# Turning a column of 256 numbers into a row: tensor-engine transposes replaced by a VectorE block transpose and two trips through DRAM

## What is computed

```python
# layer 0
h = relu(layernorm(x))
weight = adj * exp((h @ Wq.T + bq) @ (h @ Wk.T + bk).T)
weight = weight / weight.sum(axis=2, keepdims=True)
x = x + weight @ (h @ Wv.T + bv)
# layer 1
h = relu(layernorm(x))
A_hat = adj + eye
d_inv_sqrt = A_hat.sum(axis=-1) ** -0.5
L = A_hat * d_inv_sqrt[:, :, None] * d_inv_sqrt[:, None, :]
x = x + L @ (h @ W + b)
```

## Time and profile before

| | |
|---|---|
| median of 3 runs | 1750.32 us (1748.71 to 1751.24) |
| the profiled execution, its own time | 1750.99 us |
| its span in the trace, first to last instruction | 1749.1 us |
| TensorE busy | 1725.3 us (99%) |
| VectorE busy | 1266.5 us (72%) |
| ScalarE busy | 746.5 us (43%) |
| GpSimd busy | 555.7 us (32%) |
| DMA | 105.55 MB, mean 60 GB/s |
| mean granted TensorE clock | 0.997 of full speed |

### The profile page before, as it was taken

One profiled execution on the slowest core, in us unless ns is written; L12 is line 12 of the kernel. 1 busy time (PEld: TensorE's weight loads), 2 busy tenths in 40 slices (PEclk: granted clock), 3 DMA queues, 4 the chain that ended last, 5 costly groups with the idle time before them and its releaser, 6 DMA issues.

```text
span 1749.1 us, 32667 instructions
## 1 busy us (share of the span) xinstructions
PE 1725.3 (99%) x11452; PEld 1574.7 (90%) x11452; DVE 1266.5 (72%) x3097; ACT 746.5 (43%) x1546; POOL 555.7 (32%) x585
## 2 busy tenths in 40 slices
PE   7999999999999999999999999999999999999997
PEld 5899999999999999999999999999999999999996
DVE  5677777777777777777767777777777777777774
ACT  3444344353444444444443443534444444434432
POOL 1323323323323323333233233233233233332331
PEclk9999999999999999999999999999999999999999
DMA  5212212212122122122122121121221221221210
GB/s 157 61 43 66 69 39 72 60 48 72 54 54 72 54 54 72 48 60 71 41 68 67 41 72 55 53 72 54 54 72 51 57 72 43 65 69 39 72 48 25
DMA packets 191978, 105.55 MB, mean 60 GB/s; under 512 B 140512, under 2 KB 156896, under 8 KB 191968
## 3 DMA queue, kind: packets, MB, share of 16 engines
q1 hardware_dynamic: 190048, 103.84, 21.0%
q10 hardware_dynamic: 1920, 1.58, 0.3%
HBM read 71.83 MB, written 33.55 MB: 60 GB/s over the span
## 4 chain that ended last, share of the span: by engine, by line
PE 98%; DVE 1%; issue 0%; ACT 0%; DMA 0%; POOL 0%; ACTq 0%; POOLq 0%; DVEq 0%
PE ps L546 31%; PE ps L548 31%; PE ps L547 31%; PE ps L630 3%; PE ps L556 1%; PE ps L613 1%; DMA late<-in_L_gnn_Wq_w_dram 0%; ACT late L287 0%; DVE p_lo L515 0%; ACT h_hi L289 0%; DVE z_lo L486 0%; DVE late L492 0%; DVE w_in L395 0%; DVE wvt_lo L385 0%; POOL hat_lo L227 0%
## 5 line engine op out<-in xcount | busy, mean ns | idle before, releaser
L287 ACT ACTIVATE late<-late,nb,sc 128x512 f32<-128x512 f32 x128 | 103.6, 809 | 587.5 <-DVE nb L443 587.5
L546 PE MATMUL ps<-ht_hi,m_hi 128*128 128x256 f32 x1024 | 287.3, 281 | 0.8 <-DVE wvt_lo L385 0.8
L547 PE MATMUL ps<-ht_lo,m_hi 128*128 128x256 f32 x1024 | 288.0, 281 | 0.0
L548 PE MATMUL ps<-ht_hi,m_lo 128*128 128x256 f32 x1024 | 287.5, 281 | 0.0
L224 POOL TENSOR_TENSOR hat_hi<-adjt,eye 128x512 fp32r<-128x512 f32 x64 | 82.7, 1293 | 580.4 <-DVE p_lo L515 580.4
L546 PE MATMUL ps<-w_hi,z_hi 128*128 128x512 f32 x512 | 207.7, 406 | 1.5 <-DVE z_lo L486 1.5
L548 PE MATMUL ps<-w_hi,z_lo 128*128 128x512 f32 x512 | 202.4, 395 | 0.0
L547 PE MATMUL ps<-w_lo,z_hi 128*128 128x512 f32 x512 | 202.3, 395 | 0.0
L546 PE MATMUL ps<-wvt_hi,ht_hi 128*128 128x512 f32 x512 | 202.2, 395 | 0.0
L548 PE MATMUL ps<-wvt_hi,ht_lo 128*128 128x512 f32 x512 | 202.1, 395 | 0.0
L547 PE MATMUL ps<-wvt_lo,ht_hi 128*128 128x512 f32 x512 | 202.0, 395 | 0.0
(11 more groups left out here) (102 smaller groups left out, 4529.1 us busy)
## 6 DMA issues: line engine op xcount, KB each, us to landing
x_in<-in_x_dram SPq DMA_DIRECT2D x64, 512.0 KB, 3.5
out_dram<-late SPq DMA_DIRECT2D x128, 256.0 KB, 2.0
adj_in<-in_adj_dram SPq DMA_DIRECT2D x64, 256.0 KB, 2.8
adj_blocks<-in_adj_dram SPq DMA_DIRECT2D x256, 64.0 KB, 2.8
late<-in_L_gnn_Wk_w_dram SPq DMA_DIRECT2D x4, 256.0 KB, 4.9
late<-in_L_gnn_Wq_w_dram ACTq DMA_DIRECT2D x4, 256.0 KB, 7.7
wv_in<-in_L_gnn_Wv_w_dram SPq DMA_DIRECT2D x1, 1024.0 KB, 7.9
w_in<-in_L_gnn_W_dram SPq DMA_DIRECT2D x1, 1024.0 KB, 7.7
```

The costliest lines, as they stand in the source:

```text
L287: act.activation(h1[:, t, :], x1[:, t, :], ACT.Relu, scale=sc_1[:, t:t + 1], bias=nb_1[:, t:t + 1])
L546: pe.matmul(dst, a_hi[:, c, cols], b_hi[:, c, :], start=(c == 0), stop=False)
L547: pe.matmul(dst, a_hi[:, c, cols], b_lo[:, c, :], start=False, stop=False)
L548: last = pe.matmul(dst, a_lo[:, c, cols], b_hi[:, c, :], start=False, stop=(c == chunks - 1))
```

## The change

`dn` becomes the first two columns of a tile `dn_wide` of 128 by 32, cleared once at the start. Each step, VectorE transposes `dn_wide` in blocks of 32 by 32 into `dn_turned`: then partition `32 q + t` holds the 32 numbers of nodes `128 t + 32 q` to `128 t + 32 q + 31`. SP stores these eight pieces of 128 bytes to a scratch tensor in DRAM, by two DMAs of four pieces. When they have landed, it loads the 1 KB back to all 128 partitions as `dn_row`, in one DMA, and VectorE's row sum reads `dn_row` from SBUF in place of bank 7. The two transposes on TensorE and the waits around them go.

```diff
@@ sync
                 if main and ahead:
                     sp.wait_ge(adjt_ready, this)
                     load_blocks(sp, adj_next)
+                if main:
+                    sp.wait_ge(dn_turned_ready, this)
+                    if prev:
+                        sp.wait_ge(dn_row_loaded, (this - 1) * 16)
+                    for t in range(NT):
+                        sp.dma_start(dn_dram[t], dn_turned[t::32, :]).then_inc(dn_stored, 16)
+                    sp.wait_ge(dn_stored, this * (16 * NT))
+                    if prev:
+                        sp.wait_ge(s_sum_ready, this - 1)
+                    sp.dma_start(dn_row[:], dn_dram.rearrange("t q c -> (t q c)").partition_broadcast(P)).then_inc(
+                        dn_row_loaded, 16)
                 if prev:
@@ gpsimd
+            pool.memset(dn_wide[:], 0.0)
...
                         pool.wait_ge(d_ready, this - 1)
+                        pool.wait_ge(dn_turned_ready, this - 1)
@@ vector
                 if main:
+                    dve.wait_ge(dn_ready, this)
+                    if prev:
+                        dve.wait_ge(dn_stored, (this - 1) * (16 * NT))
+                    dve.transpose(dn_turned[:], dn_wide[:]).then_inc(dn_turned_ready, 1)
+                if main:
                     for j in range(2):
                         dve.wait_ge(g_hi_ready[j], this)
...
-                    dve.wait_ge(dn_row_done, this)
+                    dve.wait_ge(dn_row_loaded, this * 16)
...
-                            out=unused_a[:, t, :], in0=adj_kept[:, t, :], in1=ps[:, DR, 0:N], scale=1.0,
+                            out=unused_a[:, t, :], in0=adj_kept[:, t, :], in1=dn_row[:], scale=1.0,
@@ tensor
-                    pe.wait_ge(dn_ready, this)
-                    if prev:
-                        pe.wait_ge(x1_ready[0], this - 1)
-                    for t in range(NT):
-                        last = pe.transpose(ps[:, DR, t * P:(t + 1) * P], dn[:, t:t + 1].to_broadcast([P, P]), ident[:])
-                    last.then_inc(dn_row_done, 1)
                     pe.wait_ge(g_lo_ready[1], this)
...
-                    pe.wait_ge(s_sum_ready, this)
+                    if prev:
+                        pe.wait_ge(x1_ready[0], this - 1)
```

More of the change, by code:

```diff
@@ L62, in gnn_program @@
         adj_blocks = sb("adj_blocks", [P, NT, N])
+        dn_row = sb("dn_row", [P, N])
+        dn_wide, dn_turned = sb("dn_wide", [P, 32]), sb("dn_turned", [P, 32])
+        dn_dram = nc.dram_tensor("dn_scratch", (NT, P // 32, 32), fp32, kind="Internal").ap()
         h = sb("h", [P, NT, D])
@@ L96, in gnn_program @@
         rsum, rsum1 = sb("rsum", [P, NT]), sb("rsum1", [P, NT])
-        dn, d = sb("dn", [P, NT]), sb("d", [P, NT])
+        dn, d = dn_wide[:, 0:NT], sb("d", [P, NT])
         rinv = sb("rinv", [P, NT])
@@ L101, in gnn_program @@
         ps = ctx.enter_context(nc.psum_tensor("ps", [P, 8, 512], fp32))
-        G, Z, HT, V, O1, DR = 0, 2, 2, 4, 4, 7
+        G, Z, HT, V, O1 = 0, 2, 2, 4, 4
         O = (6, 2)
@@ L130, in gnn_program @@
         blocks_loaded, adjt_ready = sem("blocks_loaded"), sem("adjt_ready")
-        dn_row_done = sem("dn_row_done")
+        dn_turned_ready, dn_stored, dn_row_loaded = sem("dn_turned_ready"), sem("dn_stored"), sem("dn_row_loaded")
         ht_done, ht_hi_ready, ht_lo_ready = sems("ht_done"), sems("ht_hi_ready"), sems("ht_lo_ready")
```

## The result

The changed kernel takes 1735.12 us (median of 4 runs, 1733.49 to 1737.29), against 1750.65 us for the kernel before (4 runs, 1748.71 to 1751.24). The ratio is 0.9914, with a 95% interval of 0.9897 to 0.9931: faster by 0.9%. A second comparison, with 5 and 15 runs, gave 0.9924 (0.9911 to 0.9938). The profiled execution after took 1737.29 us with a span of 1735.4, 13.7 us less than that of before.

The account below looks back on a forecast made before the run. TensorE was taken to bound the loop, busy for the whole 26.57 us period. From 1750.3 us, 63 removed pairs at 0.22 (13.9) go and 0.4 in step 1 is added: 1736.8 us, range 1733.8 to 1741.5.

Parts of the forecast that it names:

- The bound: In the loop: TensorE is busy for the whole 26.57 us period and sets the time; 26.35 us expected after.
- The price of a pair: Two TensorE transposes at L613 per graph: 0.22 us of room by neighbours' starts, 64 x 0.22 = 14.1 us in all.
- What is added: VectorE's block transpose (0.2 us), unchanged row sum and DRAM round trip in the loop: all hidden, row 4.2 us early.
- Step 1: First step: the pair's 0.22 us is waited away, and a row landing at 44.3 to 44.8 costs 0.4 us.
- The sum: Whole program: 1750.3 - 13.9 + 0.4 = 1736.8 us, 0.8% faster; chance 0.82.
- the slack behind the row sum: Loop, row sum to O product: a row landing before about 869.4, 11.5 us after dn_turned, costs nothing.
- Rival 1: Loop: the row comes late in every graph and TensorE stops before O; 1794 us with 6 us hops; chance 0.04.
- Rival 2: Loop: nothing gained, another result such as z_lo is already just in time; about 1750 us; chance 0.04.
- rival 3: TensorE: the removed transposes cost their whole duration, 128 x 0.27 = 35 us; time 1716 us; chance 0.02.
- rival 4: Step 1: store queues longer or broadcast load is slow, p_lo pushed 2.6 us, half clock follows; 1739 to 1741.5; chance 0.08.

Follow-up runs that it names:

- e4: Kernel before, with the pair of TensorE transposes made four times, eight transposes in place of two; 1790.51 us, ratio 1.0238.
- e2: Changed kernel without VectorE's block transpose, the two stores and the load; the row sum reads a row of ones; 1733.99 us, ratio 0.9914 to the kernel before.
- e1: The changed kernel again without edit, timed in more rounds; 1736.46 us, ratio 0.9924 to the kernel before.
- e5: Changed kernel with the load of the row made three times in sequence in every step but the first; 1776.79 us.
- e8: Changed kernel with the load of the row made twice in sequence in every step but the first; 1735.45 us, ratio 0.9921 to the kernel before.
- e6: Changed kernel with the load of the row made four times in sequence in every step but the first; 1991.03 us, ratio 1.138 to the kernel before.
- e9: Changed kernel with three loads in sequence and VectorE's block transpose moved up behind nb_1, ahead of both h_lo, in every step but the first; 1736.74 us, ratio 0.9929.
- e7: Changed kernel with the row's trip put ahead of the four block loads on SP in step 1 only; 1735.13 us, ratio 0.9920 to the kernel before.

## Why the prediction was right, point by point

**The bound.** TensorE sets the period, and the period went from 26.57 to 26.34 us (26.35 forecast). Right.

**The price of a pair.** 0.22 us read from starts; 0.233 is the difference of the two periods, and 0.218 what each added pair costs in e4. The term was 0.013 us too small, 0.8 us over the program. The duration of 271 ns would have given 35 us; e4 rules that out (41.7 us against 104), and with it the use of the Trainium skill's 275 ns ("TensorE: Matmul & The Clock Gate", Part 4: PE-mode transpose) as the room that a transpose takes in a filled TensorE. That figure is a duration, of a bf16 transpose in another kernel. The eight transposes of `h` that remain still last 273 ns; eight of them take 0.87 us of room, 109 ns each.

**What is added.** The block transpose takes 204 ns (0.2 forecast) and costs nothing. The row sum takes 484 ns from SBUF against 478 from the accumulator bank (no change forecast). In the loop step read, the load is issued 2.5 us after the block transpose starts, and the row lands 5.4 us after it; the forecast's 5.3 counted from the transpose's end, so 5.5 from its start. The two issues took longer than forecast (1.16 us for 0.8) and the second store landed sooner, so that two small errors cancelled. VectorE comes for it 4.4 us later (4.2 forecast). e2 shows the trip to be free in the loop.

**Step 1.** The row was forecast at 44.3 to 44.8 and landed at 44.94 on a clock that was 0.24 us behind. The chain of the changed kernel in step 1 runs through SP's queue as foretold:

```profile
39.45 0.63 SPq L204
...
40.13 1.85 DMA dn_scratch<-dn_turned
41.99 2.95 DMA dn_row<-dn_scratch
...
44.97 0.48 DVE w_in L521
...
45.98 0.76 DVE p L530 x2
```

`p` was pushed by 0.37 us in the profiled execution (0.4 forecast), and by 0.1 in e1. TensorE's wait for `p_lo` is about as long as before (2.2 after 2.1) and did not grow to the 2.7 that were forecast, because 0.6 us of the pause come earlier, ahead of the transposes of `h`: TensorE reaches them 0.22 us sooner, and `h` was some 0.3 us later, behind an `x_in` that landed later.

**The sum.** 13.5 us forecast, 13.7 between the profiled executions, 13.3 to 15 by the two ratios. From the periods, 63 x 0.233 = 14.7 us less 0.1 to 0.4 in step 1 are 14.3 to 14.6. So the forecast was about 1 us short of the gain, within what the runs of this kernel scatter. The range's lower end, too, was worked out a little short: 1736.8 less 1.3, 0.4 and 1.6 is 1733.5, not 1733.8.

**What was wrong: the slack behind the row sum.** The prediction let the row be late until 869.4, 11.5 us after the block transpose ends and 11.7 after it starts, by counting from the row sum to `p_lo` and from there to the O product. The trips of e5 took 11.2 to 11.9 us from the start, most of them inside that limit, and the time grew by 41.7 us. The step that failed is "the row sum itself is not yet the deadline": the row sum pushes all that follows in VectorE's queue, and by way of GpSimd's additions the next block transpose too, so a lateness that one step forgives adds up over the steps. By the ring the limit is a trip of 10.7 us; the runs place it between 8.5 (e8, free) and 11.2 (e5, not free). The forecast did not hang on it, since the trip took 5.4.

**Rivals.** None occurred. Rival 1 (a late row in each step) is real, but needs a trip twice as long. It was right in kind, wait and lower clock together (e6); that it decides at 869.4 was wrong, as said above. Rival 2 fell with the period, rival 3 with e4. Of rival 4 the profiled execution had the 0.4 us that were in the sum.

## What to carry to other kernels

In a TensorE without pauses, price an instruction by the distance of its neighbours' starts and multiply by its count; a change that takes it away and puts the work on engines and queues with room gives about that product (13.9 us by the rows read ahead, 14.7 by the periods). The DRAM round trip of 5 us was free here, where its result is wanted 10 us later, but the room for it is not the distance to the next deadline alone: follow the delayed engine's queue around to the place where the next trip starts, and compare the ring's length with the period. Where a ring is too long, an instruction moved up in its queue can be worth as much as a faster transfer.

## What the runs showed of the hardware

**A VectorE copy that stands still beside a GpSimd instruction.** In e5, the copy `d<-dn_wide` of 128 by 2 takes 1098 ns at the median, and 169 in every step of the changed kernel. In the ring's step it starts at 891.14, while GpSimd's `xb` (128 by 512, twice in the row) runs from 889.68 to 892.22, and it ends at 892.25 (GpSimd's rows, VectorE's row, then the copy in the changed kernel):

```profile
889.68 2.54 POOL L256 TENSOR_TENSOR xb<-x_in,bv_row 128x512 f32<-128x512 f32 x2
892.68 0.70 POOL L260 TENSOR_TENSOR rs<-ve,minus_half 128x2 f32<-128x2 f32 x1 [0.46 <-DVE ve L457]
...
891.14 1.11 DVE L452 COPY d<-dn_wide 128x2 f32<-128x2 f32 x1
...
L447 DVE COPY d<-dn_wide x64: 169/169/170, 55.6 to 1714.1; 128x2 f32<-128x2 f32 x64
```

It ends with GpSimd's instruction to 0.03 us, and in the step before to 0.02 (865.09 and 865.07). VectorE's two statistics instructions ahead of it lie wholly beside `xb` and take the 1.28 us that they take elsewhere. Behind the copy stand the mean and the variance that GpSimd's `rs` waits for, so that GpSimd idles 0.46 us after `xb`: up to that much of the 15.67 us is this copy (not tested apart). The Trainium skill ("SBUF — State Buffer", Who interferes with whom) describes a pair of ports that GpSimd shares with VectorE's copies in their fast mode, which whoever comes first holds for its whole instruction while the other is fully blocked; these rows agree with it, though no run took the GpSimd instruction away. In the changed kernel VectorE reaches the copy at another moment, 0.05 us before `xb` ends (845.78 and 845.83), and the cost doesn't show.

**The lower clock after the pause of step 1 comes and goes.** The changed kernel's profiled execution ran at 0.50 for about three microseconds after the pause, as the kernel before:

```profile
49.00:50.00 1.00, 1.00 (x5) 1.00 (x6) 0.96 (x2) 0.00 (x0) 1.00 (x1) 0.50 0.00 0
```

The same kernel in e1, after a pause of the same length, did not (the first row lies in the pause, the second behind it):

```profile
45.00:46.00 1.00, 0.00 (x0) 0.00 (x0) 1.00 (x5) 1.00 (x3) 0.00 (x0) 1.00 0.00 0
...
47.00:48.00 1.00, 1.00 (x11) 1.00 (x10) 0.70 (x2) 0.00 (x0) 1.00 (x2) 1.00 0.12 16
```

All eleven profiled executions have a pause of 2.1 to 2.6 us there. The clock fell to 0.50 behind it in five (before, the first of the changed kernel, e5, e6, e9) and stayed at 1.00 in six (e1 to e4, e7, e8); the length of the pause does not tell them apart, since it is 2.1 us in three of the five and in three of the six. From the first matmul of O to the first of the next product are 4.29 us in the changed kernel's first profiled execution (48.81 to 53.10) and 2.98 in e1 (46.56 to 49.54), so the lower clock is worth 1.3 us. In e9 it lasted longer, from 47 to 53, and the same stretch took 5.31 us (47.42 to 52.73), 2.3 more than in e1. Between the first two, SP came to its first load of step 1 at 35.71 and at 33.72, 2.0 apart. Together, these 2.0 and the 1.3 are 3.3 of the 3.4 us between the spans of two profiled executions of the changed kernel, 1735.4 and 1732.0: a difference of this size between single runs says nothing about a change.
